# A three-layer interaction tower: x0diag behind x1's copy, both rounds of x0's transposes in one PSUM bank

## What is computed

```python
def _cin_forward(X0, Ws):
    F_ = X0.shape[1]
    Xk = X0
    outs = []
    for W in Ws:                                  # 64 units each
        H_prev = Xk.shape[1]
        Wr = W.reshape(F_, H_prev, W.shape[1])
        Xk = jnp.einsum('bfd,bhd,fho->bod', X0, Xk, Wr)
        outs.append(Xk.sum(axis=2))
    return jnp.concatenate(outs, axis=1)
...
h = jnp.concatenate([z, dense_ctx], axis=1)
h = jnp.maximum(h @ W_top1 + b_top1, 0.0)
h = jnp.maximum(h @ W_top2 + b_top2, 0.0)
y = h @ W_top3
```

## Time and profile before

| | us |
|---|---|
| median of 3 runs | 496.67 |
| lowest, highest | 495.9, 500.04 |
| the profiled execution | 493.39 |
| its span, first to last instruction | 491.4 |
| around the span | 2.0 |
| mean granted TensorE clock | 0.965 |

### The profile page before, as it was taken

The page is one execution under the profiler, slowest core; times in us unless marked ns, Lnnn a source line. Parts: engine busy times, 40 slices in busy tenths (PEclk is TensorE's granted clock), DMA queues, the critical chain, the costliest instruction groups (busy, mean ns, idle before and its releaser), DMA issues.

```text
span 491.4 us, 6759 instructions
## 1 busy us (share of the span) xinstructions
PE 400.8 (82%) x2520; PEld 151.3 (31%) x2520; DVE 306.0 (62%) x305; ACT 127.8 (26%) x228; POOL 182.4 (37%) x196
## 2 busy tenths in 40 slices
PE   0008858979897889788979797988798888999997
PEld 0003112212332234222432242324232333344554
DVE  1013259968667957697669766884689458993000
ACT  1003003033241322323241314122413240125433
POOL 5777777777774575037702770000000000000000
PEclk9999969979999989999999989998999899999999
DMA  6000286047606520456025701770067007620000
GB/s 190 7 7 7 63 192 151 7 100 171 135 7 158 163 81 7 111 138 146 7 75 141 177 7 31 180 174 0 21 171 185 7 0 192 145 48 1 0 1 2
DMA packets 20757, 41.86 MB, mean 85 GB/s; under 512 B 6379, under 2 KB 9891, under 8 KB 20740
## 3 DMA queue, kind: packets, MB, share of 16 engines
q1 hardware_dynamic: 14596, 40.05, 32.9%
q0 software_dynamic: 6144, 1.59, 3.5%
HBM read 37.41 MB, written 4.20 MB: 85 GB/s over the span
## 4 chain that ended last, share of the span: by engine, by line
PE 66%; ACT 11%; DVE 7%; issue 7%; POOL 4%; DMA 4%; DVEq 0%; SPq 0%; ACTq 0%
PE acc L557 36%; PE spread L531 11%; PE misc L597 5%; DVE pairs L365 5%; ACT x0diag L432 5%; POOL emb L337 4%; ACT common L419 3%; PE spread L700 3%; PE misc L591 2%; DMA units<-x_dram 2%; PE misc L587 2%; ACT x0parts L419 2%; PE spread L694 2%; PE spread L696 1%; DVE z L370 1%
## 5 line engine op out<-in xcount | busy, mean ns | idle before, releaser
L365 DVE TENSOR_TENSOR pairs<-spread,units 128x1024 f32<-128x1024 f32 x192 | 224.4, 1217 | 36.0 <-PE spread L531 25.6
L337 POOL DMA_INDIRECT emb<-in_tbl,ids_sb x192 | 182.2, 949 | 113.4 <-issue 57.3
L557 PE MATMUL acc<-pairs,w_sb 128*64 128x512 f32 x768 | 203.6, 635 | 6.8 <-DVE pairs L365 6.6
L531 PE MATMUL spread<-x0parts,sel 72*128 72x512 bf16 (+2 forms) x224 | 73.3, 413 | 34.9 <-DVE pairs L365 22.3
L365 DVE TENSOR_TENSOR pairs<-spread,common 120x1024 f32<-120x1024 f32 (+1 forms) x48 | 58.5, 1221 | 46.8 <-PE spread L531 41.3
L557 PEld LDWEIGHTS acc<-pairs,w_sb 128*64 128x64 f32 x768 | 46.8, 140 | 91.6 <-issue 67.5
L557 PE MATMUL acc<-pairs,w 120*64 120x512 f32 (+1 forms) x180 | 51.5, 652 | 0.0
L531 PEld LDWEIGHTS spread<-x0parts,sel 72*128 72x128 bf16 (+2 forms) x224 | 17.9, 118 | 109.1 <-DVE pairs L365 49.7
L419 ACT ACTIVATE x<-acc 128x512 f32<-128x512 f32 x31 | 18.8, 606 | 90.6 <-PE acc L557 90.6
L432 ACT ACTIVATE x0diag<-misc,mask 128x384 f32<-128x384 f32 x64 | 31.7, 610 | 25.5 <-PE misc L582 25.5
L579 PE MATMUL misc<-ident_b,parts 128*72 128x128 bf16 x64 | 5.5, 233 | 38.9 <-DVE parts L289 38.9
(11 more groups left out here) (37 smaller groups left out, 148.4 us busy)
## 6 DMA issues: line engine op xcount, KB each, us to landing
units<-x_dram SPq DMA_DIRECT2D x64, 512.0 KB, 7.3
x_dram<-x SPq DMA_DIRECT2D x32, 128.0 KB
emb<-in_tbl,ids_sb POOLq DMA_INDIRECT x192
w_sb<-in_w SPq DMA_DIRECT2D x2, 384.0 KB
wt_sb<-in_wt SPq DMA_DIRECT2D x1, 512.0 KB, 5.6
wt1a_sb<-in_wt1a SPq DMA_DIRECT2D x1, 256.0 KB, 4.5
wt1b_sb<-in_wt1b SPq DMA_DIRECT2D x1, 160.0 KB, 5.1
sel<-in_sel SPq DMA_DIRECT2D x1, 124.9 KB
```

The costliest lines, as they stand in the source:

```text
L337: pool.indirect_dma_start(out=e3[:, f, :], out_offset=None, in_=tables[f], in_offset=bass.IndirectOffsetOnAxis(ap=ids_sb[:, t, f:f + 1], a ...
L365: dve.tensor_tensor(pairs[buf][0:rows, :], source[0:rows, :], other[0:rows, h * HALF:(h + 1) * HALF], ALU.mult).then_inc(pairs_done, 1)
L531: last = pe.matmul(spread[ring][0:rows, half * BLK:(half + 1) * BLK], sel[:, first:first + rows], src[:, cols(h, half)], start=True, stop= ...
L557: last = pe.matmul(acc[half * H:(half + 1) * H, :], w, pairs[buf][0:rows, half * BLK:(half + 1) * BLK], start=first, stop=final)
```

## The change

`SIDE` gets new places: xt at 1 and 3 (before: 3 and 5), x2t's first round at 6 (7), z3 at 19 (23), x0t at 21 (19). So x0t stands behind z3, and at ACT behind x1's copy. The common spreads stand at 5 and 8 (6 and 9). In step 0 xt stands at 6 and 8 (7 and 8) and x0t at 22 (23). Both rounds of the transposes use `misc`; `acc1` takes round 1 for the very first tile alone, ahead of step 0. Round 1 waits for the copy of round 0 and no longer for `z1_done`.

```diff
-SIDE = {3: ("xt", 0), 5: ("xt", 1), 7: ("x2t", 0), 9: ("x2t", 1), 11: ("gram", 0), 13: ("gram", 1),
-        15: ("gram", 2), 17: ("gram", 3), 19: ("x0t", 0), 23: ("z3", 0)}
-SIDE_FIRST = {7: ("xt", 0), 8: ("xt", 1), 23: ("x0t", 0)}
+SIDE = {1: ("xt", 0), 3: ("xt", 1), 6: ("x2t", 0), 9: ("x2t", 1), 11: ("gram", 0), 13: ("gram", 1),
+        15: ("gram", 2), 17: ("gram", 3), 19: ("z3", 0), 21: ("x0t", 0)}
+SIDE_FIRST = {6: ("xt", 0), 8: ("xt", 1), 22: ("x0t", 0)}
...
-MIDDLE = Plan((11, 14, 16, 21, 23, 27), (6, 9), (0, 1), SIDE, 0)
+MIDDLE = Plan((11, 14, 16, 21, 23, 27), (5, 8), (0, 1), SIDE, 0)
...
-        xt_bank = [bank[0:FP, :].bitcast(BF16) for bank in (misc, acc1)]
+        def xt_bank(tile, r):
+
+            return (acc1 if r and isinstance(tile, int) and tile == 0 else misc)[0:FP, :].bitcast(BF16)
...
             def side_waits(number, what, i):
-                if what == ("xt", 1):
-
-                    pe.wait_ge(z1_done, 2 * i + 2)
-                else:
-
-                    after(pe, misc_free, number)
+                after(pe, misc_free, number)
```

More of the change, by code:

```diff
@@ L427, in take @@
                     copy(x0parts[1 - slot][:, :].rearrange("p (k d r) -> p d k r", d=D, r=8)[:, r * 8:(r + 1) * 8],
-                         xt_bank[r].rearrange("p (d k r) -> p d k r", d=8, r=8)).then_inc(misc_free, 1)
+                         xt_bank(i + 1, r).rearrange("p (d k r) -> p d k r", d=8, r=8)).then_inc(misc_free, 1)
                 elif kind == "x0t":
@@ L469, in _ @@
             copy(ident_b[:, :], ident[:, :]).then_inc(const_done, 1)
-            take(0, ("xt", 0), 1, 0)
-            take(1, ("xt", 1), 1, 0)
+            take(0, ("xt", 0), 1, -1)
+            take(1, ("xt", 1), 1, -1)
             for h in range(2):
@@ L578, in side_round @@
                     for d in range(8):
-                        last = pe.transpose(xt_bank[r][:, d * P:(d + 1) * P], parts[:, r * 8 + d, :], ident_b[:, :])
+                        last = pe.transpose(xt_bank(i + 1, r)[:, d * P:(d + 1) * P], parts[:, r * 8 + d, :], ident_b[:, :])
                 elif kind == "x0t":
```

## The result

| | before | changed |
|---|---|---|
| median of 4 runs, us | 498.36 | 462.35 |
| lowest, highest | 495.9, 502.86 | 461.58, 464.28 |
| the profiled execution | 493.39 | 462.07 |
| its span | 491.4 | 459.8 |

The ratio is 0.9292 with a 95% interval of 0.9256 to 0.9327. A kernel's median is over all its runs, while every ratio leaves out the slow ones of both kernels, so the two need not fit exactly. The forecast was 468.4 in a range of 460 to 478, faster with a chance of 0.96.

What follows compares the result with a forecast made beforehand. PE was taken as the bound. 3.73 us a step times six is 22.4; with the corrections for single steps 21.8, plus 6.5 from the clock, 28.3. 496.67 - 28.3 = 468.4 us, range 460 to 478.

Steps and rivals of the forecast that it cites:

- What bounds the kernel: Middle steps: PE sets the pace, busy 82% of the span; its idle time and low clock can be won.
- x1's copy: Ahead of item 23's spread: x1's copy before x0diag's fill removes PE's wait, 3.04 us a step; still late 8%.
- T: Start of x0t in the old kernel's profiled step, 297.54, where z3 stands instead; zero point of the walk.
- The common copies: Common spreads at 5 and 8: PE's waits of 1.60 and 0.55 us go, 2.15 us a step won.
- The transposes: Two rounds sharing misc: the sum's 1.28 us wait goes, new waits of 1.00 and 1.74 us add 2.74.
- The rule weighed against the trace: Rotating matmul groups through PSUM banks speaks against both rounds in misc; price here about 0.5 us a step.
- The sum of a step: Middle step: 3.04 + 2.15 + 1.28 - 2.74 = 3.73 us won without the clock; with 1.68 more, 45.8 us.
- Step 0: First step: x0t and round 0 moved earlier, net 0.6 us won, plus 1.5 us from less low clock.
- Step 7 and the tail: Last step: x0t two places later, its fill still covered; 0 change, at most 0.5 us lost.
- The clock: Low clock in two of six middle steps, 5.0 us won; with step 0, 6.5, between -1.7 and +11.5.
- no drop would come at all: Rival: waits this short cost no clock, so no low clock anywhere, 463.4 us; chance 20%.
- The offset: Median of the runs lay 3.3 us above the profiled execution; the forecast was taken from the median, 496.67.

Runs made afterwards that it cites:

- h1: g3 with x2t's first round at 7 instead of 6; full-clock step 44.32 us against the changed kernel's 45.13, whole run 626.73 us, ratio 0.933, on a disturbed chip.
- f3: Changed kernel with x2's second copy on ACT moved behind the copy of round 0; steps 43.46 and 43.47 us, whole run 615.87 us, ratio 0.917.
- g1: Changed kernel with f3's ACT order, xt at 2 and 3, z3 at 20, x0t at 22; step 43.09 us, whole run 449.44 us, ratio 0.9035.
- the second trace: The changed kernel measured again, unedited; 461.54 us, ratio 0.927, steps of 45.13 and 45.14 us, one low-clock step of 46.78 us.
- e3: Kernel before with only the second common spread moved from 9 to 8; full-clock step 47.43 us, whole run 653.77 us, ratio 0.995.
- f2: Same kernel as e3, run again; steps 5 and 6 took 49.02 and 50.23 us with low clock, whole run 657.21 us, ratio 0.978.
- f4: f3 with xt at 2 and 4 and the first common spread at 6; steps 44.69 and 44.68 us, whole run 624.47 us, ratio 0.930.
- g3: Changed kernel with round 1 of the transposes in acc1 at place 5, first common spread at 6; steps 47.70 us, whole run 474.11 us, ratio 0.946.
- e1: Kernel before with only z3 at 19 and x0t at 21; 3.11 us a step less, whole run 640.63 us, ratio 0.976.

## Why the prediction was right

- **What bounds the kernel**: as said. 31.3 of the 31.6 us between the two spans are in the middle steps, out of PE's waits, its low clock and, a smaller part, its pace.
- **x1's copy**: 3.04 us a step forecast, 3.11 measured alone. The walk was right to a few hundredths: x1's copy at T + 2.50 (2.55), PE at the spread at T + 5.44 (5.30), no wait.
- **The common copies**: the spreads' waits went, as forecast; the second alone was worth 2.10 us instead of 1.60 (1.68 by the distance of starts).
- **The transposes**: 2.74 us of new waits forecast; 0.91 + 1.72 = 2.63 by the distance of starts (202.80 to 204.62 less one contraction; 205.19 to 208.73 less two). Against that stand 1.28 + 0.55 saved. So this part loses by itself, by 0.9 us a step in the forecast. The runs agree: a full-clock step less the two other parts, 49.53 - 3.11 - 2.10 = 44.32, against 45.13 in the changed kernel, is 0.8 lost. This is a difference of runs; no run has the two other parts together and the transposes as before. The change wins in spite of it.
- **The rule weighed against the trace**: I put the price of giving up the second bank at about 0.5 us a step; h1 gives 0.81. The Trainium skill (Perfetto Trace Analysis, Matmuls) was right in sign. But f3 with one bank is 0.86 us better than h1 with two: where the copy can be hidden by its place in ACT's queue, the second bank is not needed. In g1, with one contraction between the rounds, the one bank still costs 0.27 us; f3's order on ACT with two banks was not run.
- **The sum of a step**: 3.73 and, with the low clock gone, 5.41 forecast; 51.21 to 45.13 is 6.08. Most mis-sized are the removed waits. I took them from the brackets, which count from the modelled end of the last matmul, and the new ones from the distance of starts, about 0.1 us a piece more. By starts the three removed waits are 3.16, 1.39 and 1.68, together 0.3 more. The new waits were 0.1 less than forecast. The rest, some 0.25, is pace: contractions that follow each other take 0.91 us and not 1.01, a round of x2t followed by a spread 0.50 and not 0.58. In step 1 I took 1.2 us off, since the sum's wait is nearly absent there; the new wait for the split is absent there too, so only 0.5 came off (3.94 us won, where a full-clock step wins 4.40).
- **Step 0**: 0.6 us of gain and 1.5 us from the clock forecast, 0.1 measured. The last low stretch did shrink, from 6.8 us (inside the 7.2 of the earlier trace rows) to 3.4, but round 0, which now stands ahead of c3, lets PE stand idle for 4.36 us at the split instead of 1.86 (75.13 in the changed kernel, where 75.97 in the earlier trace rows), and a low stretch from 73.9 to 80.8 begins in this wait. The kernel before had one from 64.2 to 74.6, the changed one 63.6 to 70.6. All low stretches of step 0 together are 17.1 us in both, so the clock gave nothing back. The wait was not only moved past one contraction; it was put in one piece.
- **Step 7 and the tail**: 0 forecast, 0.2 gained; behind the fill and the two zin_b copies 0.29 us of cover were left.
- **The clock**: two of six steps forecast with a low clock, two found, one in the second trace. That was luck in part: the reading under it, that the 1.60 us wait brings the drop and the 3.04 us one doesn't, fell with e3 and f2. What decides whether a given wait is followed by a drop stays open. That no drop would come at all, as the Trainium skill (TensorE: Matmul & The Clock Gate, HAM oscillation) has it for short gaps, fell as well: one follows 1.60 us in both traces of the changed kernel.
- **The offset**: the runs of before scatter from 495.9 to 502.9 and their median lies 5 us above the profiled execution; those of the changed kernel lie within 2.7 us of each other, and their median is that of the profiled one. I had carried the offset over unchanged (3.3 us), which makes half of the 6 us by which the forecast was high. The other half has both signs in it: the middle steps won 5 us more than forecast, step 0 won 2 less. The measured 462.35 lies 2.4 us above the lower end of the range; had step 0 won its 2 us too, it would stand at the very edge. That it does not is luck. Fewer low-clock stretches are a likely reason for the smaller scatter; no run here shows it.

## What to carry to other kernels

In a kernel of hand-ordered engines, look at each long copy or fill on the engine that empties PSUM (ACT here) and ask what short, urgent copy is queued behind it: moving eight activations behind one gave 3.1 us a step without removing an instruction. Check the new order on that engine too, not on the matmul engine alone: two items at the same place cost 1.6 us in f4 and g3, exactly the fault that the change had mended elsewhere. And compare waits by the distance of starts, removed and added ones alike.

## What the runs showed of the hardware

- The low clock is not tied to one wait of a program. In the same program form (the changed kernel) it followed a wait of 1.60 us in two steps of six in one trace and in one of six in another, and with the kernel before's 1.60 us wait removed (e3, f2) it came with one of 3.04 us, which had never brought it in the six steps of the trace of before. Behind g3's wait of 1.60 us, ahead of a spread, it came in six steps of six; behind f4's wait at the same place in neither of the two steps compared. Nor does it begin at a fixed distance: 1.0 us behind the end of the wait in step 4 of the kernel before, 1.7 behind in step 3 of the changed one, 0.8 before the end in step 6 of f2. With no wait much above 0.5 us in a middle step (g1) there was none.
- A stretch of 3.4 us costs 1.6 to 1.7 us of a step (e1, f2, the changed kernel). One of 6.8 us cost 2.8 us (e3, f2), less than double, since there its first 0.8 us fell into PE's own wait.
- On three of the four chips of the experiments the kernel before took about 170 us more than on the other, by stalls of up to 36 us on several engines in steps 0 to 4. The last of them end within 6 us of the last gather of POOL, but gathers run in the undisturbed traces too, and what the engines waited for stays open. Since each chip was used at one time only, the runs don't tell the chip from the time.
